# A feed-forward layer of inner width 682 in eleven tiles of up to 128 instead of twelve of 114, in a kernel whose engines follow orders written out by hand

## Chip, cores and metric

The kernel runs on one core of a Trainium2 chip, as one program. The metric is the time of one execution on the device in microseconds. Engines are called by the profile's names: PE (TensorE, with PEld for its weight loads), DVE (VectorE), ACT (ScalarE), POOL (GpSimd), SP (the queue that issues DMAs).

## What is computed

The input is x of shape 8 x 1024 x 256 in float32. A differential attention with 16 heads and a layer norm come first; the change doesn't touch them. Then follow two layers of local attention and gated feed-forward, and another layer norm. Cut to what matters:

```python
for l in range(2):
    h = shift_token(x)                       # half of the channels one token later
    q, k, v = split(h @ wqkv)                # 8 heads of 64
    q, k = rotary_xpos(l2norm(q) * q_scale, l2norm(k) * k_scale)
    x = x + local_attention(q, k, v) @ wo    # windows of 128 tokens, each sees itself and the one before
    h = shift_token(x)
    h = (h - mean) / sqrt(var + 1e-5) * ln_g + ln_b
    a, g = split(h @ w1 + b1)                # 256 -> 2 x 682
    x = x + (a * gelu(g)) @ w2 + b2          # 682 -> 256
```

682 is 6 x 113.67, or 5 x 128 + 42.

## The kernel before

The first half of the program (to about 2950 us of the span) is the differential attention. The second half walks 128 windows W of 128 tokens: 2 layers x 8 sequences x 8 windows. Four windows make a half sequence of 512 tokens, and the feed-forward of half m runs beside the attention of the four windows that follow it, spread by c = W % 4:

- c = 0: attention_out (8 matmuls, x = x + o @ wo), mean
- c = 1: variance, then gate tiles 0 to 5 (2 matmuls each, 256 = 2 x 128 rows of contraction)
- c = 2: hidden tiles 0 to 5 (2 matmuls each); ACT takes the gelu of the gates between two table loads, DVE multiplies (gated)
- c = 3: ffn_out (2 x 6 matmuls)

So windows 0 to 3 run with no feed-forward beside them, and the last half's feed-forward runs alone after window 127.

Beside this each window W does its attention: queries and keys of window W + 1 (PSUM banks 0 and 1), values of W, four head pairs hp of scores (banks 4 and 5), a maximum on DVE (largest), exp and sum on ACT (exps), a division on DVE (normalise), a transposition on PE (transpose_p, bank 3), a copy to SBUF on ACT (place_p), and the weighing of the values on PE (weigh, bank 6). Queries and keys of W + 1 are squared on ACT (squares), normed (DVE norms, ACT inverse_norms, POOL), rotated on DVE (rotate_own, rotate_other, combine), transposed on PE (transpose_q, transpose_k, again bank 3) and copied by ACT (place_q, place_k). In the first window of a sequence (W % 8 = 0) the keys are 128 instead of 256, so that scores, transpositions, copies and weighing have half the columns or half the calls.

Nothing schedules this: each engine runs its own attend(W) (PE from L945, ACT from L1366, DVE from L1782), a list of calls for each c, written out by hand, and every engine takes its list strictly in order. Waits are on semaphores. Those that matter here:

```python
pe.wait_ge(t_read, done(W * 6 + 2 + hp))     # transpose_p: ACT has copied bank 3 after the transposition before
pe.wait_ge(t_read, done(W * 6 + 1))          # transpose_k: place_q is done
pe.wait_ge(t_read, done(W * 6 + 2))          # scores(W, 0): place_k of this window is done
pe.wait_ge(p_ready, done(W * 4 + hp + 1))    # transpose_p: DVE's normalise
pe.wait_ge(xsum_done, done(m + 1))           # mean: POOL has summed the two residuals
pe.wait_ge(hn_done, done(2 * m + 2))         # gate 0: scale_bias on ACT
```

Feed-forward results and values take turns in PSUM banks 7 and 2: fbank(use) gives the bank of the use-th result of a half, 22 uses in a half. gate (L892) writes ps[0:114], gate_out on ACT (L1338) copies it with the bias to gates, gelu works in place, hidden (L912) writes ps[0:114], gated on DVE (L1761) adds the bias and multiplies, ffn_out (L929) contracts 114 rows at a time. w1 lies as [128, 2, 2, 6, 114], w2 as [114, 6, 256], padded from 682 to 684.

Of the kernel before, what the change touches and what calls it, by code (L numbers as in the profile page):

```python
# [6 lines left out]
F32 = mybir.dt.float32  # L7
# [32 lines left out]
HP = -(-HID // HB)  # L40
# [3 lines left out]
def done(n):  # L44

    return n + START
# [70 lines left out]
def fbank(use):  # L117

    return 2 if use % 2 else 7


V_USE = (0, 5, 12, 19)
# [7 lines left out]
def program(nc, d, nb):  # L130

    assert nb % 2 == 0
    with ExitStack() as ctx:
# [79 lines left out]
        w1 = sb("w1", [P, 2, 2, HB, HP], F32)  # L213
        w2 = sb("w2", [HP, HB, 256], F32)
# [3 lines left out]
        b1 = sb("b1", [HP, 2, HB], F32)  # L218
# [20 lines left out]
        gb_ = sb("gates", [HP, HB, 512], F32)  # L239
        hh = sb("hh", [HP, HB, 512], F32)  # L240
# [299 lines left out]
        def _(pe):  # L540
# [319 lines left out]
            def attention_out(m, oc, fs, beside):  # L860
# [19 lines left out]
            def mean(m):  # L880
# [3 lines left out]
                pe.matmul(ps[:, fbank(3), :], mean_w[:], both[:, 0, :], start=True, stop=True).then_inc(fm_full, 1)  # L884

            def variance(m):
# [3 lines left out]
                pe.matmul(ps[:, fbank(4), :], mean_w[:], both[:, 1, :], start=True, stop=True).then_inc(fv_full, 1)  # L890

            def gate(m, j, beside, kcs=(0, 1)):  # L892
# [14 lines left out]
                for kc in kcs:  # L907
                    mmi = pe.matmul(ps[0:HP, fbank(6 + j), :], w1[:, kc, 1, j, :], cn[:, kc, :], start=kc == 0, stop=kc == 1)  # L908
# [3 lines left out]
            def hidden(m, j, beside, kcs=(0, 1)):  # L912
# [11 lines left out]
                for kc in kcs:  # L924
                    mmi = pe.matmul(ps[0:HP, fbank(13 + j), :], w1[:, kc, 0, j, :], cn[:, kc, :], start=kc == 0, stop=kc == 1)  # L925
# [3 lines left out]
            def ffn_out(m, oc, js, beside):  # L929
# [7 lines left out]
                for j in js:  # L937
                    mmi = pe.matmul(ps[:, fbank(20 + oc), :], w2[:, j, oc * P:(oc + 1) * P], hh[:, j, :],  # L938
# [4 lines left out]
            def attend(W):  # L943
                m, c = half_of(W), W % 4
                if c == 0:  # L945
# [16 lines left out]
                    attention_out(m, 1, (1,), True)  # L962
                    weigh(W, 0)
                    weigh(W, 1)
                    transpose_p(W, 2)
                    attention_out(m, 1, (2,), True)
                    transpose_p(W, 3)
                    attention_out(m, 1, (3,), True)
                    transpose_q(W + 1)
                    weigh(W, 2)  # L970
                    weigh(W, 3)
                    transpose_k(W + 1)
                    mean(m)
                    scores(W + 1, 0)
                elif c == 1:
                    queries(W + 1, 0)
                    queries(W + 1, 1)
                    scores(W, 1)
                    keys(W + 1, 0)
                    variance(m)  # L980
                    keys(W + 1, 1)
                    transpose_p(W, 0)
                    scores(W, 2)
                    values(W, 0)
                    values(W, 1)
                    transpose_p(W, 1)
                    scores(W, 3)
# [3 lines left out]
                    weigh(W, 0)  # L991
                    weigh(W, 1)
                    transpose_p(W, 2)
# [3 lines left out]
                    transpose_p(W, 3)  # L997
                    gate(m, 3, True, (0,))
                    gate(m, 3, True, (1,))
                    gate(m, 4, True, (0,))  # L1000
                    gate(m, 4, True, (1,))
                    transpose_q(W + 1)
                    gate(m, 5, True, (0,))
# [1088 lines left out]
```

## Time and profile before

| what | us |
|---|---|
| median of 3 runs (6137.58 to 6144.04) | 6137.9 |
| the profiled execution's own time | 6143.95 |
| its span, first to last instruction | 6141.9 |
| PE busy | 5830.0 (95%) |
| DVE busy | 4145.9 (68%) |
| ACT busy | 3460.2 (56%) |
| POOL busy | 910.1 (15%) |
| mean granted TensorE clock | 0.983 |

The span is what lies between the first and the last instruction; the execution's own time has some 2 us more. Busy shares are averages over both halves of the program. The end of a matmul is modelled, so that busy time of PE tells less than the distance between starts. A timeline row merges a run of like instructions: start, duration of the run, engine, line, operation, names, shapes, xcount, and in brackets the idle time before it and what ended it. A float32 matmul makes two records (x2); a transposition of a head pair makes four, a scores call four, a weigh call eight. "issue" is time in which an engine waited for nothing that the profile shows.

### The profile page before, as it was taken

Reading aid. Unit: us, or ns where it says so; the run is one execution under the profiler, and the core shown is the slowest. Engines: PE = TensorE matmul, PEld = TensorE weight load, DVE = VectorE, ACT = ScalarE, POOL = GpSimd, SP = SyncE. Lnnn points to the kernel's source line nnn. Section 1 sums busy time; section 2 is a strip of 40 time slices with the busy share of each in tenths; the row PEclk is TensorE's granted clock in tenths of the full one; section 3 lists DMA queues with packets and bytes.
Section 4 is the critical chain, followed back from the end, with each engine's and each line's share of the span. In section 5 each row is a group of like instructions: output and inputs, shape, how many; then the busy total and the mean of one; then the engine's idle time right before and its main releaser. Section 6 shows DMA issues by size and latency. Waiting matters only on the chain.

```text
span 6141.9 us, 146596 instructions
## 1 busy us (share of the span) xinstructions
PE 5830.0 (95%) x58112; PEld 2637.5 (43%) x58112; DVE 4145.9 (68%) x10780; ACT 3460.2 (56%) x6980; POOL 910.1 (15%) x1873
## 2 busy tenths in 40 slices
PE   8999999999999999998699999999999999999985
PEld 3343434344343434433344444444444444444432
DVE  5777777777777777775566666666666666666633
ACT  4666666666666666665355555555555555555532
POOL 2222222222222222211000000000000000000000
PEclk9999999999999999999799999999999999999997
DMA  3333333332323333231100000000000000000004
GB/s 67 52 52 61 52 61 51 57 57 49 66 51 62 51 56 57 48 60 33 64 8 14 15 8 14 14 8 15 12 27 15 11 11 15 11 11 15 11 28 144
DMA packets 137129, 232.17 MB, mean 38 GB/s; under 512 B 40476, under 2 KB 40604, under 8 KB 135680
## 3 DMA queue, kind: packets, MB, share of 16 engines
q1 hardware_dynamic: 136448, 222.83, 17.5%
q8 instruction: 460, 7.54, 0.5%
q14 instruction: 221, 1.81, 0.1%
HBM read 53.86 MB, written 33.55 MB: 14 GB/s over the span
## 4 chain that ended last, share of the span: by engine, by line
PE 81%; issue 6%; DVE 6%; ACT 4%; DMA 2%; POOL 1%; SPq 0%; POOLq 0%; ACTq 0%; DVEq 0%
PE ps L548 21%; PE ps L677 14%; PE ps L769 12%; PE ps L908 5%; PE ps L938 5%; PE ps L925 5%; PE ps L835 5%; PE ps L855 4%; PE ps L843 4%; ACT pt L1179 3%; DVE mc L1542 2%; PE ps L875 2%; PE ps L813 1%; PE ps L822 1%; DVE junk L1538 1%
## 5 line engine op out<-in xcount | busy, mean ns | idle before, releaser
L1179 ACT ACTIVATE pt<-ps 128x1024 f32<-128x1024 f32 (+7 forms) x2048 | 1235.7, 652 | 747.5 <-PE ps L548 525.5
L1538 DVE CUSTOM_DVE_ANT_0 junk<-ps,causal 128x128 bf16<-128x128 f32 (+3 forms) x2048 | 989.2, 487 | 439.7 <-PE ps L548 422.7
L548 PE MATMUL ps<-kt,qt 96*32 96x512 bf16 (+3 forms) x12288 | 1066.9, 332 | 100.0 <-DVE mc L1542 55.8
L677 PE MATMUL ps<-pt,ones 128*32 128x512 f32 (+3 forms) x6144 | 1151.1, 489 | 0.0
L677 PE MATMUL ps<-pt,vs 128*32 128x512 f32 (+3 forms) x3072 | 1147.6, 489 | 0.0
L677 PE MATMUL ps<-pt,va 128*32 128x512 f32 (+3 forms) x3072 | 1144.2, 487 | 0.5 <-POOL pt L1952 0.4
L548 PE MATMUL ps<-qt,kt 98*32 98x512 bf16 (+3 forms) x12288 | 827.9, 328 | 42.0 <-ACT pt L1179 32.7
L769 PE MATMUL ps<-wqkv,xs 128*128 128x512 f32 x1536 | 786.1, 621 | 13.8 <-DMA wqkv<-in_wqkv 13.8
L1542 DVE TENSOR_REDUCE mc<-ps 128x1 f32<-128x512 f32 x1024 | 704.8, 688 | 99.7 <-PE ps L548 77.0
L1952 POOL TENSOR_SCALAR_AFFINE_SELECT pt<-pt 128x256 f32<-128x256 f32 x1024 | 454.9, 444 | 2139.2 <-ACT pt L1179 2139.2
L548 PEld LDWEIGHTS ps<-kt,qt 96*32 96x32 bf16 x12288 | 347.9, 94 | 893.9 <-DVE mc L1538 429.4
L1301 ACT ACTIVATE sm<-sm,mxw 128x256 f32<-128x256 f32 (+1 forms) x1024 | 495.4, 485 | 335.0 <-DVE mxw L1719 334.6
L1719 DVE CUSTOM_DVE_ANT_0 sm<-ps,window 128x256 f32<-128x256 f32 (+1 forms) x1024 | 375.7, 405 | 321.9 <-PE ps L835 320.2
L1309 ACT ACTIVATE ptw<-ps 128x512 f32<-128x512 f32 (+1 forms) x512 | 287.4, 561 | 442.5 <-PE ps L843 413.4
L548 PEld LDWEIGHTS ps<-qt,kt 98*32 98x32 bf16 x12288 | 331.1, 96 | 337.4 <-issue 161.1
L677 PEld LDWEIGHTS ps<-pt,va 128*32 128x32 f32 x3072 | 320.0, 109 | 311.3 <-issue 187.1
L1979 POOL TENSOR_TENSOR nt<-rn 128x16 f32<-128x16 f32 x128 | 44.2, 345 | 2403.9 <-ACT rn L1278 2403.9
L769 PEld LDWEIGHTS ps<-wqkv,xs 128*128 128x128 f32 x1536 | 257.8, 191 | 276.6 <-issue 269.0
L938 PE MATMUL ps<-hh,w 114*128 114x512 f32 x768 | 363.5, 597 | 0.9 <-DVE hh L1768 0.9
L908 PE MATMUL ps<-cn,w 128*114 128x512 f32 x768 | 354.8, 599 | 4.4 <-ACT cn L1335 4.4
L925 PE MATMUL ps<-cn,w 128*114 128x512 f32 x768 | 358.0, 596 | 0.8 <-ACT gates L1345 0.8
L835 PE MATMUL ps<-kp,qp 64*128 64x256 f32 (+1 forms) x2048 | 348.7, 417 | 7.0 <-DVE mxw L1719 4.2
(147 smaller groups left out, 8570.0 us busy)
## 6 DMA issues: line engine op xcount, KB each, us to landing
qt<-part SPq DMA_DIRECT2D x768, 64.0 KB, 2.4
kt<-part SPq DMA_DIRECT2D x768, 64.0 KB, 2.5
ya<-wy SPq DMA_DIRECT2D x128, 128.0 KB, 2.3
yb<-wy SPq DMA_DIRECT2D x128, 128.0 KB, 2.3
xs<-between_phases SPq DMA_DIRECT2D x32, 512.0 KB, 3.9
between_phases<-xo SPq DMA_DIRECT2D x32, 512.0 KB, 2.8
xt<-in_x SPq DMA_DIRECT2D x16, 512.0 KB, 6.0
between_phases<-z SPq DMA_DIRECT2D x16, 512.0 KB, 2.8
```

The source lines that it names most:

```text
L548: mmi = pe.matmul(ps[32 * q:32 * q + 32, bank, lo:hi], weights[:, 32 * q:32 * q + 32], moving, start=start, stop=stop)
L677: mmi = pe.matmul(ps[32 * q:32 * q + 32, 4 + half, lo - half * 512:hi - half * 512], w, probs(kb)[:, i, lo - first(kb):hi - first(kb)], st ...
L769: return pe.matmul(ps[:, bank, :], xs[:, kc, at:at + P], wqkv[l][:, kc, n * 512:n * 512 + 512], start=kc == 0, stop=kc == 1)
L835: pe.matmul(ps[:, 4 + q, 0:n], qp[rows, hp, :], kp[rows, hp, :, :].rearrange("p a k -> p (a k)")[:, 0:n], start=True, stop=True).then_inc( ...
L908: mmi = pe.matmul(ps[0:HP, fbank(6 + j), :], w1[:, kc, 1, j, :], cn[:, kc, :], start=kc == 0, stop=kc == 1)
L925: mmi = pe.matmul(ps[0:HP, fbank(13 + j), :], w1[:, kc, 0, j, :], cn[:, kc, :], start=kc == 0, stop=kc == 1)
L938: mmi = pe.matmul(ps[:, fbank(20 + oc), :], w2[:, j, oc * P:(oc + 1) * P], hh[:, j, :], start=j == 0, stop=j == HB - 1)
L1179: act.activation(probs(kb)[:, i, kb * P - first(kb):1024 - first(kb)], ps[:, 2 * i:2 * i + 2, :].rearrange("p a q -> p (a q)")[:, kb * P:1 ...
L1301: i = act.activation(sm[:, hp, q, 0:n], sm[:, hp, q, 0:n], ACT.Exp, scale=-1.0, bias=mxw[:, hp, q:q + 1], accum_out=sumw[:, hp, q:q + 1])
L1538: ins = dve.tensor_tensor_reduce(out=junk[:, bank - 6, 0:w], in0=ps[:, bank, 0:w], in1=causal[:, 512 - w:512], scale=1.0, scalar=NEG, op0= ...
L1542: ins = dve.reduce_max(into, ps[:, bank, 0:w], AX_X)
L1952: pool.affine_select(out=diag, in_=diag, compare_op=ALU.is_ge, fill=0.0, base=0, pattern=[[0, 2], [1, P]], channel_multiplier=-1).then_inc ...
```

## The change

The inner width is cut into 5 tiles of 128 and one of 42. The five full tiles have a gate and a hidden matmul pair each as before. The last tile has its 42 hidden values and its 42 gates in one tile of w1: hidden values on rows 0 to 41, gates on rows 64 to 105 (HPAIR = 106), so that one pair of matmuls makes both; it is called gate 5, and hidden 5 is gone. ACT copies all 106 rows with their bias, takes the gelu of rows 64 to 105 into a tile of its own (glast, rows 0 to 41), and DVE multiplies the two in SBUF. ffn_out contracts 128 rows five times and 42 rows once. A half has now 21 results in PSUM, an odd number, so the turn of the banks depends on m as well. b1, w1 and w2 are laid out on the host to match.

Cut to its core (the changes of fbank's arguments and of the layout on the host are left out):

```diff
-HP = -(-HID // HB)
+HLAST = HID - (HB - 1) * P
+HPAIR = 64 + HLAST
...
-def fbank(use):
-
-    return 2 if use % 2 else 7
...
-V_USE = (0, 5, 12, 19)
+def fbank(m, use):
+
+    return 2 if (m + use) % 2 else 7
...
+V_USE = (0, 5, 12, 18)
...
-        w1 = sb("w1", [P, 2, 2, HB, HP], F32)
-        w2 = sb("w2", [HP, HB, 256], F32)
+        w1 = sb("w1", [P, 2, 2 * HB - 1, P], F32)
+        w2 = sb("w2", [P, HB, 256], F32)
...
                 for kc in kcs:
-                    mmi = pe.matmul(ps[0:HP, fbank(6 + j), :], w1[:, kc, 1, j, :], cn[:, kc, :], start=kc == 0, stop=kc == 1)
+                    if j < HB - 1:
+                        mmi = pe.matmul(ps[:, fbank(m, 6 + j), :], w1[:, kc, j, :], cn[:, kc, :], start=kc == 0, stop=kc == 1)
+                    else:
+                        mmi = pe.matmul(ps[0:HPAIR, fbank(m, 6 + j), :], w1[:, kc, 2 * HB - 2, 0:HPAIR], cn[:, kc, :],
+                                        start=kc == 0, stop=kc == 1)
...
                 for j in js:
-                    mmi = pe.matmul(ps[:, fbank(20 + oc), :], w2[:, j, oc * P:(oc + 1) * P], hh[:, j, :],
+                    rows = slice(0, P if j < HB - 1 else HLAST)
+                    mmi = pe.matmul(ps[:, fbank(m, 19 + oc), :], w2[rows, j, oc * P:(oc + 1) * P], hh[rows, j, :],
                                     start=j == 0, stop=j == HB - 1)
...
-            for j in range(HB):
+            for j in range(HB - 1):
                 hidden(m, j, False)
...
+                if j < HB - 1:
+                    act.activation(gb_[:, j, :], gb_[:, j, :], ACT.Gelu).then_inc(ge_done, 1)
+                else:
+                    act.activation(glast[:, :], gb_[64:HPAIR, j, :], ACT.Gelu).then_inc(ge_done, 1)
...
+                if j < HB - 1:
+                    dve.wait_ge(a_full, done(m * (HB - 1) + j + 1))
+                    dve.scalar_tensor_tensor(hh[:, j, :], ps[:, fbank(m, 13 + j), :], b1[:, HB - 1 + j:HB + j], gb_[:, j, :],
+                                             ALU.add, ALU.mult).then_inc(hh_done, 1)
+                else:
+                    dve.tensor_tensor(hh[0:HLAST, j, :], gb_[0:HLAST, j, :], glast[:, :], ALU.mult).then_inc(hh_done, 1)
...
```

The lists of calls of PE, ACT and DVE are written anew for all four c. On DVE, in c = 3, heads_out and output change places at the end, so that the two outputs come first. Three places of the built programs show the rest.

PE at the end of c = 0, from the last attention_out (L875, in the change L877) to the first scores of the next window (L835, L837). L843/L845 is transpose_p, L855/L857 weigh (x4 for each head pair), L813/L815 transpose_q, L822/L824 transpose_k, L884/L886 the mean. Before:

```order
L875 MATMUL ps<-ot,wo 128x512 x5
L855 MATMUL ps<-ptw,vt 64x128 x8
L843 MATMUL ps<-identf,sm 128x128 x4
L875 MATMUL ps<-ot,wo 128x512
L843 MATMUL ps<-identf,sm 128x128 x4
L875 MATMUL ps<-ot,wo 128x512
L813 MATMUL ps<-identf,rr 128x128 x4
L855 MATMUL ps<-ptw,vt 64x128 x8
L822 MATMUL ps<-identf,rr 128x128 x4
L884 MATMUL ps<-both,mean_w 128x512
L835 MATMUL ps<-kp,qp 128x256 x2
```

And in the change:

```order
L877 MATMUL ps<-ot,wo 128x512 x8
L845 MATMUL ps<-identf,sm 128x128 x4
L857 MATMUL ps<-ptw,vt 64x128 x8
L845 MATMUL ps<-identf,sm 128x128 x4
L857 MATMUL ps<-ptw,vt 64x128 x4
L815 MATMUL ps<-identf,rr 128x128 x4
L886 MATMUL ps<-both,mean_w 128x512
L824 MATMUL ps<-identf,rr 128x128 x4
L857 MATMUL ps<-ptw,vt 64x128 x4
L837 MATMUL ps<-kp,qp 128x256 x2
```

The eight attention_out matmuls now stand together, the mean has moved between the two last transpositions, and between transpose_p 3 and transpose_q, and between transpose_k and the scores, there is one weigh call and no 512-column matmul.

PE in the second half of c = 2, from the last long run of hidden matmuls on (L925, in the change L931). Before:

```order
L925 MATMUL ps<-cn,w_93 114x512 x3
L855 MATMUL ps<-ptw,vt 64x128 x8
L843 MATMUL ps<-identf,sm 128x128 x4
L925 MATMUL ps<-cn,w_93 114x512
L843 MATMUL ps<-identf,sm 128x128 x4
L925 MATMUL ps<-cn,w_93 114x512
L813 MATMUL ps<-identf,rr 128x128 x4
L855 MATMUL ps<-ptw,vt 64x128 x8
L822 MATMUL ps<-identf,rr 128x128 x4
L925 MATMUL ps<-cn,w_93 114x512
L835 MATMUL ps<-kp,qp 128x256 x2
```

And in the change:

```order
L931 MATMUL ps<-cn,w_93 128x512 x3
L857 MATMUL ps<-ptw,vt 64x128 x4
L845 MATMUL ps<-identf,sm 128x128 x4
L931 MATMUL ps<-cn,w_93 128x512 x2
L845 MATMUL ps<-identf,sm 128x128 x4
L857 MATMUL ps<-ptw,vt 64x128 x4
L845 MATMUL ps<-identf,sm 128x128 x4
L857 MATMUL ps<-ptw,vt 64x128 x4
L815 MATMUL ps<-identf,rr 128x128 x4
L931 MATMUL ps<-cn,w_93 128x512
L824 MATMUL ps<-identf,rr 128x128 x4
L857 MATMUL ps<-ptw,vt 64x128 x4
```

Hidden 5 is gone. Two gaps between transpositions (2 and 3, 3 and q) that held a hidden matmul now hold a weigh call of one head pair (x4), and one such call stands between transpose_k and the scores.

ACT in c = 2, from the inverse norms on: L1350/L1359 and L1360/L1372 are the table loads, L1356/L1366 and L1368 gelu, L1309/L1314 place_p, L1301/L1306 exps (x2 a head pair). Before:

```order
L1278 ACTIVATE rn_108<-lnn 128x16
L1350 ACT_TABLE_LOAD
L1356 ACTIVATE gates<-gates 114x512 x5
L1309 ACTIVATE ptw<-ps 128x512
L1356 ACTIVATE gates<-gates 114x512
L1360 ACT_TABLE_LOAD
L1301 ACTIVATE sm,sumw<-sm,mxw 128x256 x2
L1309 ACTIVATE ptw<-ps 128x512
L1301 ACTIVATE sm,sumw<-sm,mxw 128x256 x2
L1309 ACTIVATE ptw<-ps 128x512 x2
L1289 ACTIVATE qp<-ps 128x512
L1295 ACTIVATE kp<-ps 128x4x128
```

And in the change:

```order
L1283 ACTIVATE rn_108<-lnn 128x16
L1359 ACT_TABLE_LOAD
L1366 ACTIVATE gates<-gates 128x512
L1314 ACTIVATE ptw<-ps 128x512
L1366 ACTIVATE gates<-gates 128x512 x4
L1368 ACTIVATE glast<-gates 42x512
L1372 ACT_TABLE_LOAD
L1306 ACTIVATE sm,sumw<-sm,mxw 128x256 x4
L1314 ACTIVATE ptw<-ps 128x512 x3
L1294 ACTIVATE qp<-ps 128x512
L1300 ACTIVATE kp<-ps 128x4x128
```

place_p 0 has moved ahead of five gelus, and exps 3 ahead of place_p 1, so that the three copies after it stand together.

## Rows read from the trace of the kernel before

**Rows 1.** Busy time of TensorE, from the page.

```profile
PE 5830.0 (95%) x58112; PEld 2637.5 (43%) x58112; DVE 4145.9 (68%) x10780; ACT 3460.2 (56%) x6980; POOL 910.1 (15%) x1873
```

**Rows 2.** Stretches: us, busy PE, PEld, DVE, ACT, POOL, clock, DMA.

```profile
4340.94:4362.57 21.63, 21.63 (x104) 10.54 (x103) 14.84 (x36) 9.44 (x26) 2.98 (x5) 1.00 0.15 48
4362.57:4387.01 24.44, 24.44 (x113) 12.12 (x111) 14.85 (x35) 16.51 (x37) 2.49 (x5) 1.00 0.01 2
4387.01:4410.91 23.90, 23.90 (x111) 11.29 (x109) 17.29 (x39) 15.32 (x34) 0.86 (x4) 1.00 0.01 1
4410.91:4434.41 23.50, 23.50 (x110) 11.71 (x108) 14.25 (x35) 9.63 (x26) 0.86 (x4) 1.00 0.00 1
```

**Rows 3.** Timeline of PE in c = 0.

```profile
4343.48 1.12 PE L769 MATMUL ps<-wqkv,xs 128*128 128x512 f32 x2
4344.54 0.70 PE L835 MATMUL ps<-kp,qp 64*128 64x256 f32 x4
...
4350.41 4.46 PE L875 MATMUL ps<-ot,wo 128*128 128x512 f32 x10
4354.80 1.09 PE L855 MATMUL ps<-ptw,vt 128*64 128x128 f32 x16
4355.82 0.66 PE L843 MATMUL ps<-identf,sm 128*128 128x128 f32 x4
4356.32 1.02 PE L875 MATMUL ps<-ot,wo 128*128 128x512 f32 x2
4357.26 0.63 PE L843 MATMUL ps<-identf,sm 128*128 128x128 f32 x4
4357.72 1.02 PE L875 MATMUL ps<-ot,wo 128*128 128x512 f32 x2
```

**Rows 4.** Timeline of all engines at the end of c = 2.

```profile
4404.41 0.66 PE L843 MATMUL ps<-identf,sm 128*128 128x128 f32 x4
...
4405.10 0.60 ACT L1309 ACTIVATE ptw<-ps 128x512 f32<-128x512 f32 x1 [1.53 <-PE ps L843]
4405.81 0.42 PEld L843 LDWEIGHTS ps<-identf,sm 128*128 128x128 f32 x4 [0.73 <-issue]
...
4408.83 0.66 PE L822 MATMUL ps<-identf,rr 128*128 128x128 f32 x4
...
4409.52 0.60 ACT L1295 ACTIVATE kp<-ps 128x512 f32<-128x512 f32 x1 [1.01 <-PE ps L822]
4410.27 0.30 PEld L835 LDWEIGHTS ps<-kp,qp 64*128 64x128 f32 x4 [0.77 <-ACT kp L1295]
```

**Rows 5.** Timeline of all engines around the mean, in a sequence's first window.

```profile
4450.21 0.69 DVE L1742 TENSOR_TENSOR xm<-ps,xs 128x512 f32<-128x512 f32 x1 [1.25 <-PE ps L875]
...
4450.98 1.27 POOL L1991 TENSOR_TENSOR both<-xm 128x512 f32<-128x512 f32 x1 [5.66 <-DVE xm L1742]
...
4452.30 1.12 PE L884 MATMUL ps<-both,mean_w 128*128 128x512 f32 x2 [0.35 <-POOL both L1991]
```

**Rows 6.** Groups by line, 3400 to 5800 us: the hidden matmuls.

```profile
L925 PE MATMUL ps<-cn,w 128*114 128x512 f32 x624 | 291.4, 596 | 0.0
```

**Rows 7.** Timeline of ACT in c = 2 (window from 4387.01).

```profile
4394.69 1.28 ACT L1350 ACT_TABLE_LOAD   x1
4395.99 2.71 ACT L1356 ACTIVATE gates<-gates 114x512 f32<-114x512 f32 x5
...
4401.01 0.51 ACT L1301 ACTIVATE sm<-sm,mxw 128x256 f32<-128x256 f32 x1
...
4402.01 0.57 ACT L1309 ACTIVATE ptw<-ps 128x512 f32<-128x512 f32 x1
```

**Rows 8.** Groups by line, 3400 to 5800 us: variance to normed input.

```profile
L1335 ACT ACTIVATE cn<-cn,lnp 128x512 f32<-128x512 f32 x52 | 39.6, 808 | 0.0
L1758 DVE TENSOR_TENSOR cn<-cn,rlf 128x1024 f32<-128x1024 f32 x26 | 31.9, 1225 | 11.5 <-ACT rlf L1327 11.5
L1325 ACT ACTIVATE rlf<-ps,eps_c 128x512 f32<-128x512 f32 x26 | 17.9, 688 | 0.2 <-PE ps L890 0.2
```

More of the change, by code:

```diff
@@ L883, in mean @@
                 pe.wait_ge(xsum_done, done(m + 1))
-                pe.matmul(ps[:, fbank(3), :], mean_w[:], both[:, 0, :], start=True, stop=True).then_inc(fm_full, 1)
+                pe.matmul(ps[:, fbank(m, 3), :], mean_w[:], both[:, 0, :], start=True, stop=True).then_inc(fm_full, 1)
             def variance(m):
@@ L978, in attend @@
                     scores(W, 1)
+                    variance(m)
+                    values(W, 0)
+                    values(W, 1)
+                    scores(W, 2)
                     keys(W + 1, 0)
-                    variance(m)
                     keys(W + 1, 1)
                     transpose_p(W, 0)
[L983 to L987, printed above, removed]
                     gate(m, 0, True, (0,))
@@ L996, in attend @@
                     gate(m, 2, True, (1,))
-                    transpose_p(W, 3)
+                    transpose_p(W, 1)
+                    scores(W, 3)
+                    weigh(W, 0)
+                    weigh(W, 1)
                     gate(m, 3, True, (0,))
+                    transpose_p(W, 2)
                     gate(m, 3, True, (1,))
@@ L1011, in attend @@
                     queries(W + 1, 1)
+                    keys(W + 1, 0)
+                    keys(W + 1, 1)
+                    scores(W, 1)
+                    values(W, 0)
+                    values(W, 1)
+                    hidden(m, 0, True, (0,))
+                    hidden(m, 0, True, (1,))
+                    scores(W, 2)
+                    transpose_p(W, 0)
+                    hidden(m, 1, True, (0,))
+                    hidden(m, 1, True, (1,))
+                    scores(W, 3)
+                    hidden(m, 2, True, (0,))
+                    hidden(m, 2, True, (1,))
+                    hidden(m, 3, True, (0,))
+                    weigh(W, 0)
+                    transpose_p(W, 1)
+                    hidden(m, 3, True, (1,))
+                    hidden(m, 4, True, (0,))
+                    transpose_p(W, 2)
+                    weigh(W, 1)
+                    transpose_p(W, 3)
+                    weigh(W, 2)
+                    transpose_q(W + 1)
+                    hidden(m, 4, True, (1,))
+                    transpose_k(W + 1)
+                    weigh(W, 3)
+                    scores(W + 1, 0)
+                else:
+                    queries(W + 1, 0)
+                    queries(W + 1, 1)
+                    values(W, 0)
                     scores(W, 1)
```

225 lines of the change are left out of this document (100 added, 125 removed).

## The prediction, made before the change was run

> **What bounds the kernel now.** I read the page's busy shares first: TensorE is busy 5830.0 of 6141.9 us, every other engine far less [rows 1]. A share this high can hide waits, so the view that decides is the table of stretches cut at the start of successive windows of the second half [rows 2]. There PE is busy for all of 21.63, 24.44, 23.90 and 23.50 us, at a granted clock of 1.00 (full speed, 2.4 GHz), while VectorE (DVE) has 14 to 17 us and ScalarE (ACT) 9 to 17 us of work. One feed-forward half takes four such windows, some 93 us, and 31 of the 32 halves run beside windows. The end of a matmul is modelled, though, so a busy PE may still be waiting, and only the spacing of starts tells what one call costs.
>
> That spacing is in the timeline of PE [rows 3]. One 512-column matmul (two records) is 0.86 us: five of them take 4.39 us (4350.41 to 4354.80), the last stretched 0.09 by what follows. Scores (64 rows) and weigh (64 columns) use part of the array; crossing to or from the other kind costs about 0.1 us: a 512-column matmul between two scores calls takes 1.06 (4343.48 to 4344.54), 0.2 more than inside a run. Two head pairs of weigh take 1.02 (4354.80 to 4355.82); with the records read singly 0.49 are the first's and 0.54 the last's. A transpose group costs 0.50 after weigh (4355.82 to 4356.32) and 0.46 to 0.44 after a matmul (4357.26 to 4357.72). Pricing both orders with these spacings, as if nothing waited, gives for full windows c = 0 to 3 of before 21.15, 24.43, 23.67 and 23.67 us, 92.9 together; measured were 21.63, 24.44, 23.90 and, with the cheap first scores of a sequence, 23.50 (that saves 0.21). So before waits nearly 0.5 in c = 0 and 0.2 in c = 2, and hardly elsewhere. Counting the windows at a sequence's start, whose transposes are half as long, that is about 0.9 us in a half.
>
> What are the waits? **All transposes share bank 3.** The round trip is in [rows 4]: transposes start at 4404.41, ACT copies from 4405.10 for 0.60, the next transposes' weights load at 4405.81. So two transpose groups start at least 1.43 apart after weigh, 1.38 after a matmul (4355.82 to 4357.26 is 1.44 with one matmul between, which itself then took 0.94). The keys' transposes at 4408.83, copied at 4409.52, let the next scores load at 4410.27, the same distance. One 512-column matmul between two transposes almost covers the trip; one weigh call (0.54) doesn't. The other wait is the mean in c = 0: DVE's second residual at 4450.21, the POOL sum at 4450.98, the matmul at 4452.30, with PE idle 0.35 by its own row [rows 5].
>
> **The change, part by part.**
>
> 1. Hidden tile 5 is gone, two matmuls in a half: 2 x 0.86 = 1.72 us, in 32 halves 55 us. Columns streamed set the price, so tiles of 128 instead of 114 values cost the same (the hidden group of before, on 114 columns, has 596 ns a record [rows 6], and spaces its matmuls at 0.86 like attention_out on 128), and ffn_out keeps its twelve matmuls.
>
> 2. Waitless spacing of the new order. Runs of scores or weigh calls stay 23 in a half, but three pairs of weigh calls are pulled apart (3 x 0.05), and at two borders a matmul stands where a transpose stood (2 x 0.05): +0.25. Priced as before: 21.20, 24.28, 22.21, 23.77, together 91.46, which is 1.46 less.
>
> 3. Round trips of bank 3 in the new order.
>  - c = 0 ends transpose_p 3, weigh 2, transpose_q, mean, transpose_k, weigh 3, scores. The spacing to transpose_q would be 0.55 + 0.54 = 1.09 and must be 1.43: wait 0.34. To transpose_k 0.50 + 0.86: wait 0.08. From transpose_k to scores 0.53 + 0.54 = 1.07 against 1.38: wait 0.31. Sum 0.73, where before had nearly 0.5 (one-matmul trips and the mean). The mean is no longer late: the eight attention_out calls end about 15.7 us into the window, two residuals of 0.69 and the sum of 1.27 end by 18.4, and the mean is due at 18.9.
>  - c = 1: transpose_p 3, one matmul, transpose_q, one matmul, transpose_k: 2 x 0.08.
>  - c = 2 ends transpose_p 2, weigh 1, transpose_p 3, weigh 2, transpose_q, hidden 4, transpose_k, weigh 3, scores: 0.31 + 0.34 + 0.08 + 0.31 = 1.04, where before had 0.2.
>  - c = 3: transpose_p 1, one matmul, transpose_p 2: 0.08.
>  With these the windows are 21.93, 24.44, 23.25 and 23.85 against 21.63, 24.44, 23.90 and 23.71: +0.30, 0, -0.65, +0.14. At a sequence's start (every other c = 0) the transposes are half as long and I get +0.15 for +0.30. Sum in a half: -0.28 us. **Of the 1.46 us of spacing won, 1.2 come back as waits of a transpose for a copy.**
>
> 4. Matmul ffn_out 5 now contracts 42 rows. No row of before has a 512-column matmul on so few. The nearest from one side is ffn_out on 114 rows, which passes as a full one (0 added), from the other the scores on 64 rows, which pay 0.1 at each border. 42 rows fit in 64, so I take the second: once it stands between two transposes (+0.09, +0.1 and +0.05, less the 0.08 wait of c = 3, which it covers), once ahead of scores (its border only moves). I take +0.2 in a half; ends 0 and 0.4. The Trainium skill, page TensorEngine Tiling (Array Packing), under Tiling Modes, says that changing the tiling mode, not just the tile, drains TensorE, and has a 64-row mode for contractions up to 64. By that rule the sum has this term, by the 114-row row alone it has not and would end 6 us lower.
>
> 5. ACT and DVE queues. In c = 2 exps 3 moves ahead of place_p 1 [rows 7]. From the first table load ACT must do 1.3 + six gelus at 0.54 + a copy 0.57 + 1.3 + two exps at 1.0 + the copy 0.57 = 9.0 us; the load began 7.7 us into the window before (4394.69 less 4387.01) and may begin 7.2 to 7.7 now, so the copy ends by 16.7 and transpose_p 2 is due at 16.97: covered, with 0.2 us to spare. In c = 1 the variance ends at 3.6; ln and exp (0.69 and much the same), divide (1.23) and two scalings of 0.81 with four handovers of 0.1 end at 8.2 or just before [rows 8], and gate 0 is due at 8.2: 0, at most 0.1. In c = 3 heads_out now stands behind output 1, so the next window's first maximum starts 0.7 late; scores 1 waits for it and is due 0.3 after it ends. POOL and SP get no new work; each weight load is a few kB larger and off the path. All at nothing; if a cover is gone, its microseconds go straight to PE.
>
> 6. The last half, after the windows, has no other work on PE: -1.7. Windows 0 to 3 carry no feed-forward work, 88 us of latency in a new order: 0, plus or minus 2.
>
> Sum: 31 x (-0.28 + 0.2) - 1.7 = -4.2 us. The profiled execution took 6143.95 (span 6141.9), the median of the runs is 6137.9; taken from each, 6139.8 and **6133.7**. I call a difference under 0.2% (12.3 us) no change, about what a measurement of this kernel can tell.
>
> **The rivals.**
> - *Faster: the trips are mostly hidden.* If the waits stay at before's 0.9 us a half (a copy of ACT sooner than [rows 4] have it, or PE loading weights during the trip), the gain is 31 x 1.46 + 1.7 = 47 us: 6091. If half of the new waits fall away and ffn_out 5 costs nothing, 31 x (0.28 + 0.6) + 1.7 = 29: 6109. For it: PE was full before. Against: the trip reads the same at each place. Chance of ending over 12 us faster: 0.30.
> - *Slower: ACT's queue in c = 2.* Everything from gelu 1 to exps 3 now stands ahead of place_p 1 in one queue, and transposes 2, 3, q and k and the next scores hang on it one after another. Beyond 0.2 to 0.3 us of delay it is paid whole: 1 us late is 0.7 x 31 = 22 us, so 6155. For it: the table load waits for norms on DVE behind others. Against: ACT idled over 1 us twice in that window before. Chance 0.22, with the other covers of step 5, which would show alike.
> - *The 42-row matmuls pass as full ones*: 31 x (-0.28) - 1.7 = -10.4, so 6127.5. That lies inside my own case and decides no sign alone.
>
> No change gets 0.48. Its own range is 6126 to 6150, and to hold 8 in 10 I reach to the half-way faster case and the late-ACT case: 6109 to 6156.
>
> **What the profile after would show.** Gate records 640 on 128 columns and 128 on 106, hidden 640 instead of 768, ffn_out 640 on 128 rows and 128 on 42. Window lengths cut at the wqkv matmuls: 21.9, 24.4, 23.2 and 24.0. In c = 0 and c = 2 the starts of transpose_p 3 and transpose_q 1.43 apart with one weigh call between, and transpose_k to scores 1.38. ffn_out 5: its transposes 0.53 and 0.50 if it switches the array, 0.44 if not. Wrong would be: c = 2 near 22.2 (trips hidden), transpose_p 2 in c = 2 later than 17.2 us after the window's start with ACT busy until then (the queue), or a c = 3 longer than 24.3.

## The result: 6149.8 us against 6139.6, slightly slower

| what | before | change |
|---|---|---|
| median of 20 runs, us | 6139.64 (6136.98 to 6144.04) | 6149.8 (6143.82 to 6157.67) |
| ratio, 95% interval | | 1.0016 [1.001, 1.0023] |
| profiled execution / its span, us | 6143.95 / 6141.9 | 6148.83 / 6146.8 |
| PE busy, us | 5830.0 | 5796.8 |
| mean granted clock | 0.983 | 0.985 |

PE works 33 us less by the profile's count, and the program takes 5 us more of span and 10 us more in the median. The stretches that answer to [rows 2] say where. This is the view of stretches of the change, cut at the first matmul of five successive windows: c = 0 to 3, and the c = 0 window that starts a sequence. The columns are the stretch, its us, and the busy us of PE, PEld, DVE, ACT and POOL, the granted clock, the DMA share and GB/s.

```profile
4341.25:4363.58 22.33, 21.63 (x103) 10.61 (x103) 15.91 (x38) 9.81 (x27) 3.27 (x5) 1.00 0.14 48
4363.58:4388.04 24.46, 24.46 (x112) 12.15 (x110) 14.10 (x34) 16.42 (x37) 2.13 (x5) 1.00 0.00 1
4388.04:4411.15 23.11, 22.63 (x106) 10.97 (x104) 16.92 (x39) 15.74 (x35) 0.86 (x4) 1.00 0.01 1
4411.15:4435.08 23.93, 23.93 (x111) 11.88 (x109) 13.24 (x34) 9.47 (x26) 1.95 (x4) 1.00 0.00 1
4435.08:4455.15 20.07, 19.14 (x80) 8.94 (x79) 14.18 (x38) 8.11 (x27) 3.10 (x5) 1.00 0.22 78
```

c = 2, which lost two matmuls (1.72 us), is 0.79 us shorter. c = 3 is 0.43 longer, c = 0 is 0.70 longer, and a sequence's first window 0.49 (20.07 against the 19.58 that the trace of before has from 4434.41 to 4453.99). But for a few single windows the lengths repeat to 0.02 us through the second half; c = 3 is 0.42 longer where full scores follow. In a pair of halves that is 0.70 + 0.49 - 2 x 0.79 + 2 x 0.42 + 2 x 0.02 = +0.49 us, 7.5 us over 15.5 pairs. Three single windows of before (4, 45 and 126) are together 3.8 us longer than their like and one of the change 0.3, so that windows 4 to 126 take 3.9 us more. The rest of the span's +4.9 lies around them: the second half starts 2.0 us earlier in this execution, windows 0 to 3 take 1.1 us more, and what lies behind the start of window 127 takes 2.0 us more.

The median moved by 10 us and these two executions by 5, because the one of before lies 4.3 us above its median and the one of the change 1.0 below. A single execution doesn't tell a few microseconds: over all thirteen kept traces the second half starts between 2949 and 2956 us, though the change and the edits below leave the differential attention alone. The window lengths carry the argument from here on.

The wait that I had not seen stands in c = 0. This is the timeline of all engines in the change's c = 0, from transpose_p 2 (L845) over weigh (L857), transpose_q (L815), the mean (L886) and transpose_k (L824) to the next scores (L837):

```profile
4356.85 0.60 PE L845 MATMUL ps<-identf,sm 128*128 128x128 f32 x4
...
4357.38 1.10 PE L857 MATMUL ps<-ptw,vt 128*64 128x128 f32 x16
...
4358.15 0.60 ACT L1314 ACTIVATE ptw<-ps 128x512 f32<-128x512 f32 x1 [5.50 <-PE ps L857]
...
4358.89 0.63 PE L845 MATMUL ps<-identf,sm 128*128 128x128 f32 x4 [0.41 <-ACT ptw L1314]
4359.44 0.42 PEld L857 LDWEIGHTS ps<-ptw,vt 128*64 128x64 f32 x8 [0.17 <-issue]
...
4360.29 0.63 PE L815 MATMUL ps<-identf,rr 128*128 128x128 f32 x4 [0.19 <-ACT ptw L1314]
...
4360.76 1.02 PE L886 MATMUL ps<-both,mean_w 128*128 128x512 f32 x2
...
4361.61 0.65 PE L824 MATMUL ps<-identf,rr 128*128 128x128 f32 x4
...
4362.19 0.66 PE L857 MATMUL ps<-ptw,vt 128*64 128x128 f32 x8
...
4362.95 0.30 PEld L837 LDWEIGHTS ps<-kp,qp 64*128 64x128 f32 x4 [0.34 <-ACT kp L1300]
```

transpose_q follows transpose_p 3 by 1.40 us, and the scores follow transpose_k by 1.34: the trips of [rows 4], near the 1.43 and 1.38 that were forecast. But transpose_p 3 follows transpose_p 2 by 2.04 us, though two weigh calls stand between them and only 1.43 is the trip. The bracket behind the copy at 4358.15 names who let it go: not the transposes (L845) but weigh (L857).

### The profile page after: what moved, and what is told of

Its sections match the earlier page's. It is cut to its first block, busy times and chain, and to the rows that moved or that the text cites. A ratio compares the mean times of both kernels' runs of the same rounds, so it can differ in the third digit from the quotient of the medians.

```text
span 6146.8 us, 146308 instructions
## 1 busy us (share of the span) xinstructions
PE 5796.8 (94%) x57984; PEld 2631.9 (43%) x57984; DVE 4118.5 (67%) x10780; ACT 3477.9 (57%) x6980; POOL 948.9 (15%) x1873
## 4 chain that ended last, share of the span: by engine, by line
PE 81%; DVE 6%; ACT 5%; issue 5%; DMA 2%; SPq 0%; POOL 0%; POOLq 0%; ACTq 0%; DVEq 0%
PE ps L550 21%; PE ps L679 14%; PE ps L771 12%; PE ps L945 6%; PE ps L837 5%; PE ps L911 5%; PE ps L931 4%; PE ps L845 4%; PE ps L877 3%; PE ps L857 3%; ACT pt L1184 3%; DVE mc L1554 2%; PE ps L815 1%; ACT ptw L1314 1%; PE ps L824 1%
## 5 line engine op out<-in xcount | busy, mean ns | idle before, releaser
L771 PE MATMUL ps<-wqkv,xs 128*128 128x512 f32 x1536 | 768.8, 620 | 13.9 <-DMA wqkv<-in_wqkv 13.9
L1306 ACT ACTIVATE sm<-sm,mxw 128x256 f32<-128x256 f32 (+1 forms) x1024 | 495.4, 485 | 282.0 <-DVE mxw L1731 281.6
L1314 ACT ACTIVATE ptw<-ps 128x512 f32<-128x512 f32 (+1 forms) x512 | 289.6, 566 | 522.8 <-PE ps L845 319.6
L837 PE MATMUL ps<-kp,qp 64*128 64x256 f32 (+1 forms) x2048 | 362.6, 415 | 13.1 <-ACT kp L1300 6.1
L945 PE MATMUL ps<-hh,w 128*128 128x512 f32 (+1 forms) x768 | 371.6, 609 | 1.6 <-DVE hh L1784 1.6
L1741 DVE TENSOR_TENSOR sm<-sm,sumw 128x512 f32<-128x512 f32 (+1 forms) x512 | 337.0, 658 | 17.6
L845 PEld LDWEIGHTS ps<-identf,sm 128*128 128x128 f32 x1920 | 228.7, 142 | 276.1 <-issue 240.7
```

The costliest lines, as they stand in the source:

```text
L771: return pe.matmul(ps[:, bank, :], xs[:, kc, at:at + P], wqkv[l][:, kc, n * 512:n * 512 + 512], start=kc == 0, stop=kc == 1)
L837: pe.matmul(ps[:, 4 + q, 0:n], qp[rows, hp, :], kp[rows, hp, :, :].rearrange("p a k -> p (a k)")[:, 0:n], start=True, stop=True).then_inc( ...
L845: mmi = pe.transpose(ps[:, 3, (2 * q + a) * P:(2 * q + a + 1) * P], sm[:, hp, q, a * P:(a + 1) * P], identf[:])
L945: mmi = pe.matmul(ps[:, fbank(m, 19 + oc), :], w2[rows, j, oc * P:(oc + 1) * P], hh[rows, j, :], start=j == 0, stop=j == HB - 1)
L1306: i = act.activation(sm[:, hp, q, 0:n], sm[:, hp, q, 0:n], ACT.Exp, scale=-1.0, bias=mxw[:, hp, q:q + 1], accum_out=sumw[:, hp, q:q + 1])
```

## Experiments

Windows are given as c = 0, 1, 2, 3 and, after a semicolon, a sequence's first. Before: 21.63, 24.44, 23.90, 23.50; 19.58. The change: 22.33, 24.46, 23.11, 23.93; 20.07. "Before" is a run of the kernel before on the same chip; its median lay between 6139.3 and 6142.9.

### 1. The new tiles in the old lists

```diff
 (attend of PE, ACT and DVE as before)
-                    hidden(m, 5, True, (0,))
...
-                    hidden(m, 5, True, (1,))
```

> Eleven tiles, but PE, ACT and DVE keep the lists of before, with the two calls of hidden 5 struck out; the outputs are the same. Theory A (round trips through bank 3 bound the end of c = 2): the two matmuls stood between transpose_p 3 and transpose_q and between transpose_k and the scores, where the spacing was 1.40 and 1.44 us; without them the trips still take 1.38 to 1.43 each, so c = 2 stays at 23.8 us or more (23.9 before), the other windows stay as before but for ffn_out 5 (+0.1 to 0.3 in c = 3), and the time is 6137 to 6143. Rival B (matmul time is what counts): c = 2 falls by 1.5 to 1.7 to 22.3 and the time to about 6090.

Measured: 6155.36 us, ratio 1.0019 [1.0009, 1.0028]; windows 21.63, 24.46, 23.82, 23.88; 19.58. PE at the end of its c = 2 (L931 hidden, L845 transpose_p, L815 transpose_q, L857 weigh, L824 transpose_k, L837 scores):

```profile
4412.00 0.63 PE L845 MATMUL ps<-identf,sm 128*128 128x128 f32 x4
4413.41 0.63 PE L815 MATMUL ps<-identf,rr 128*128 128x128 f32 x4 [0.78 <-ACT ptw L1314]
4413.97 1.09 PE L857 MATMUL ps<-ptw,vt 128*64 128x128 f32 x16
4414.99 0.66 PE L824 MATMUL ps<-identf,rr 128*128 128x128 f32 x4
4416.34 0.70 PE L837 MATMUL ps<-kp,qp 64*128 64x256 f32 x4 [0.69 <-ACT kp L1300]
```

With nothing between them the transposes are 1.41 us apart, and the scores 1.35 behind transpose_k. Two matmuls are gone and c = 2 is only 0.08 us shorter. Theory A's windows hold, but for c = 3, which is 0.38 longer where 0.3 was the most it allowed. All of that is in one place: the 42-row matmul stands inside a run of five ffn_out matmuls there. The run before, and the same run here (ten records in one row, under the shape of the first):

```profile
4422.72 4.56 PE L938 MATMUL ps<-hh,w 114*128 114x512 f32 x10
4428.77 4.95 PE L945 MATMUL ps<-hh,w 128*128 128x512 f32 x10
```

From its start to the next transposes it is 4.39 us before and 4.79 here. The time came out 12 us above the range named for it, with the windows adding up to +0.6 us in a pair, 10 us; as in the change, the median is some microseconds over what the windows say. So the missing matmuls give almost nothing in the old lists, and what the new lists bring in c = 2 (0.7 us) is their own.

### 2. Queries' and keys' transposes in other banks

```diff
-                pe.wait_ge(t_read, done(W * 6))
...
-                    mmi = pe.transpose(ps[:, 3, hp * P:(hp + 1) * P],     # transpose_q
+                    mmi = pe.transpose(ps[:, 0, hp * P:(hp + 1) * P],
...
-                pe.wait_ge(t_read, done(W * 6 + 1))
...
-                    mmi = pe.transpose(ps[:, 3, hp * P:(hp + 1) * P],     # transpose_k
+                    mmi = pe.transpose(ps[:, 1, hp * P:(hp + 1) * P],
...
 (place_q reads bank 0, place_k bank 1)
```

> The changed kernel with transpose_q and transpose_k written to banks 0 and 1 (queries and keys, read by then) instead of bank 3, so that they need no copy to be done first; ACT copies from there. Theory A (trips of bank 3): the waits ahead of transpose_q (0.31 in c = 0 and 2) and transpose_k (0.08) go, the trip from transpose_k to the scores stays; transpose_k comes 0.3 to 0.4 earlier, c = 0 about 22.0, c = 1 about 24.3, c = 2 about 22.85, c = 3 unchanged, the time 22 us less, about 6128. Rival B (the wait ahead of transpose_q is for combine on DVE, or ACT's copies in their order set the scores anyway): windows change by less than 0.1 and the time by less than 4 us.

Measured: 6126.51 us, ratio 0.9976 [0.9966, 0.9986]; windows 22.05, 24.30, 22.84, 23.92; 19.79. Every window is within 0.05 of theory A. The end of its c = 2 on PE (L843 transpose_p, L855 weigh, L814 transpose_q, L929 hidden 4, L822 transpose_k, L835 scores):

```profile
4392.12 0.63 PE L843 MATMUL ps<-identf,sm 128*128 128x128 f32 x4 [0.19 <-ACT ptw L1312]
4392.68 0.66 PE L855 MATMUL ps<-ptw,vt 128*64 128x128 f32 x8
4393.26 0.66 PE L814 MATMUL ps<-identf,rr 128*128 128x128 f32 x4
4393.76 1.02 PE L929 MATMUL ps<-cn,w 128*128 128x512 f32 x2
4394.62 0.60 PE L822 MATMUL ps<-identf,rr 128*128 128x128 f32 x4
4395.15 0.66 PE L855 MATMUL ps<-ptw,vt 128*64 128x128 f32 x8
4395.90 0.70 PE L835 MATMUL ps<-kp,qp 64*128 64x256 f32 x4
```

transpose_p 3 to transpose_q is 1.14 instead of 1.40, and the bracket is gone. transpose_k to the scores is 1.28 with 1.07 of work in it: that trip stays, since the scores need the copied keys.

### 3. The same banks in the old lists

```diff
 (old_orders, with transpose_q and transpose_k in banks 0 and 1)
```

> Eleven tiles in the lists of before (as in old_orders), with transpose_q and k in banks 0 and 1. Theory A (in those lists too the trips of bank 3 swallow what hidden 5 gave back): transpose_p 3 to transpose_q falls from 1.41 to about 0.44, the trip from transpose_k to the scores stays at 1.34; c = 2 falls from 23.82 to about 22.9, c = 0 by 0.1, c = 1 and 3 stay, the time by 30 us against old_orders, to about 6125. Rival B (transpose_q there waits for combine on DVE): c = 2 stays above 23.5 and the time above 6145.

Measured: 6142.48 us, ratio 1.0006 [0.9996, 1.0015]; windows 21.63, 24.45, 23.66, 23.88; 19.58. Here theory A failed: c = 2 fell by 0.16, not 0.9, and the time to 6142, not to 6125. Rival B's window (above 23.5) held, its time (above 6145) did not. transpose_q (L814) still starts 1.22 us behind transpose_p 3 at 4399.17, and its bracket names what it waits for:

```profile
4400.39 0.66 PE L814 MATMUL ps<-identf,rr 128*128 128x128 f32 x4 [0.59 <-DVE rr L1721]
```

L1721 is the last operation of combine on DVE, which in the old list stands behind normalise 3. So in the old lists two waits end within 0.2 us of each other, and sparing one leaves the other. In the new lists combine is early enough. The wait for combine was read from the trace; no run took it away by itself.

### 4. Is it normalise 3 that holds transpose_p 3?

My first reading of c = 0 was DVE's queue: combine idles 0.78 us there for POOL's norms, and normalise 3 stands behind it.

```diff
+                    normalise(W, 3)
                     combine(W + 1)
                     residual(m, 0)
-                    normalise(W, 3)
                     residual(m, 1)
```

> The changed kernel with one call moved on DVE in c = 0: normalise 3 ahead of combine and residual 0. Theory A (transpose_p 3 waits for normalise 3, which stands behind a combine that waits 0.8 us for POOL's norms): the 0.48 us wait ahead of transpose_p 3 goes, c = 0 falls from 22.33 to about 21.85 and a sequence's first window from 20.08 to about 19.6, the time by about 15 us to 6135. Rival B (the copy of bank 3 or the mean is the next to be late): c = 0 falls by less than 0.15, because the mean or transpose_q waits instead, and the time by less than 5 us.

Measured: 6150.18 us, ratio 1.001 [1.0001, 1.002]; windows 22.34, 24.46, 23.11, 23.92; 20.07. Nothing moved, so theory A fell. Rival B's number holds (less than 0.15), but not its reason, that the wait would move on to the mean or transpose_q: transpose_p 3 starts at the same point of the window, 17.64 us, as in the change. DVE's idle time was slack.

### 5. More buffers for the copied probabilities

The bracket at 4358.15 led to this. place_p(hp) writes ptw[hp % 2], the buffer that weigh(hp - 2) reads, so it waits for o_full. In the new c = 0 list weigh 0 stands behind transpose_p 2.

```diff
-        ptw = sb("ptw", [P, 2, 4, P], F32)
+        ptw = sb("ptw", [P, 4, 4, P], F32)
...
-                act.wait_ge(o_full, done(W * 4 + hp - 1))
+                act.wait_ge(o_full, done(W * 4 + hp - 3))
...
 (place_p and weigh use ptw[:, hp])
```

> The changed kernel with four instead of two SBUF buffers for the copied probabilities (ptw), so that place_p 2 and 3 need not wait for weigh 0 and 1. Theory A (in c = 0 weigh 0 now stands behind transpose_p 2, and the copy after transpose_p 2 waits for it because it writes weigh 0's buffer; transpose_p 3 waits for that copy): transpose_p 3 starts 1.55 instead of 2.04 us after transpose_p 2, c = 0 falls from 22.33 to 21.85 and a sequence's first window from 20.08 to 19.6, the other windows stay within 0.05, the time falls by 15 us to about 6135. Rival B (something else holds transpose_p 3, normalise 3 or the plain trip of bank 3): c = 0 stays within 0.1 and the time within 4 us.

Measured: 6138.91 us, ratio 0.9997 [0.9988, 1.0006]; windows 21.88, 24.46, 23.12, 23.92; 19.63. The same place in its timeline, from transpose_p 2 to transpose_p 3:

```profile
4349.57 0.60 PE L845 MATMUL ps<-identf,sm 128*128 128x128 f32 x4
...
4350.10 1.09 PE L857 MATMUL ps<-ptw,vt 128*64 128x128 f32 x16
4350.21 0.60 ACT L1314 ACTIVATE ptw<-ps 128x512 f32<-128x512 f32 x1 [4.84 <-PE ps L845]
...
4351.12 0.66 PE L845 MATMUL ps<-identf,sm 128*128 128x128 f32 x4
```

The copy now starts 0.64 us after the transposes and is let go by them (L845); transpose_p 3 follows by 1.55. c = 0 and a sequence's first window fall by 0.45 and 0.44. This one wait cost about what the whole change lost: without it the change is level with before.

### 6. The other way to take it away

```diff
                     attention_out(m, 1, (2,), True)
-                    attention_out(m, 1, (3,), True)
-                    transpose_p(W, 2)
                     weigh(W, 0)
                     weigh(W, 1)
+                    transpose_p(W, 2)
+                    attention_out(m, 1, (3,), True)
                     transpose_p(W, 3)
```

> The changed kernel with weigh 0 and 1 ahead of transpose_p 2 in c = 0, and the last attention_out matmul between transpose_p 2 and 3: the order that before had there, without a further buffer. Theory A (the copy after transpose_p 2 waited for weigh 0): transpose_p 3 follows transpose_p 2 by 1.43 instead of 2.04 us, c = 0 falls by 0.35 to 21.98 and a sequence's first window by about the same, the time by about 11 us to 6139. Rival B (mean or combine is next): c = 0 falls by less than 0.1.

Measured: 6158.0 us, ratio 1.0028 [1.0018, 1.0038]; windows 22.39, 24.46, 23.12, 23.92; 20.55. Its c = 0 (transpose_p 2 and 3, transpose_q, the mean):

```profile
4364.53 0.66 PE L845 MATMUL ps<-identf,sm 128*128 128x128 f32 x4
...
4365.97 0.63 PE L845 MATMUL ps<-identf,sm 128*128 128x128 f32 x4
4366.09 0.69 DVE L1754 TENSOR_TENSOR xm<-ps,xs 128x512 f32<-128x512 f32 x1 [0.95 <-PE ps L877]
...
4366.85 1.27 POOL L2006 TENSOR_TENSOR both<-xm 128x512 f32<-128x512 f32 x1 [4.45 <-DVE xm L1754]
4367.37 0.63 PE L815 MATMUL ps<-identf,rr 128*128 128x128 f32 x4 [0.19 <-ACT ptw L1314]
...
4368.18 1.12 PE L886 MATMUL ps<-both,mean_w 128*128 128x512 f32 x2 [0.18 <-POOL both L2006]
```

transpose_p 3 does follow by 1.44 (theory A), but the last attention_out matmul is 1.6 us later, and residual, sum and mean behind it; the mean now waits for POOL (rival B). c = 0 is 0.06 us longer than in the change, and a sequence's short first window 0.48. The wait was traded for the next one, at a loss of 8 us by the windows; the two ratios' intervals overlap.

### 7. ffn_out 5 over all rows

```diff
-                    rows = slice(0, P if j < HB - 1 else HLAST)
+                    rows = slice(0, P)
...
+            pool.memset(hh[:, HB - 1, :], 0.0).then_inc(k2_ready, 1)
```

> The changed kernel with ffn_out 5 contracting 128 rows, of which 86 are zeros (set once); all else is the same. Theory A (42 rows switch the array to its 64-row form): the transposes ahead of and behind ffn_out 5 cost 0.44 and 0.53 instead of 0.53 and 0.59, the matmul between them 0.94 (the trip) instead of 1.05, so c = 3 falls by about 0.25 to 23.87, and the time by 8 us to about 6142; at the second ffn_out 5 nothing, because it overlaps the scores now and would not then. Rival B (42 rows run like 114): no window changes by more than 0.03, time the same within 3 us.

Measured: 6143.43 us, ratio 1.0003 [0.9994, 1.0013]; windows 22.34, 24.47, 23.11, 23.70; 20.08. The change around its first ffn_out 5, and its second:

```profile
4423.63 0.60 PE L845 MATMUL ps<-identf,sm 128*128 128x128 f32 x4
4424.16 1.12 PE L945 MATMUL ps<-hh,w 42*128 42x512 f32 x2
4425.21 0.66 PE L845 MATMUL ps<-identf,sm 128*128 128x128 f32 x4
4425.80 1.09 PE L857 MATMUL ps<-ptw,vt 128*64 128x128 f32 x16
...
4432.85 1.65 PE L945 MATMUL ps<-hh,w 128*128 128x512 f32 x3
4433.81 0.49 PE L837 MATMUL ps<-kp,qp 64*128 64x128 f32 x2
4434.34 0.59 PE L945 MATMUL ps<-hh,w 42*128 42x512 f32 x1
```

And the kernel with 128 rows at the first:

```profile
4423.75 0.60 PE L845 MATMUL ps<-identf,sm 128*128 128x128 f32 x4
4424.19 1.02 PE L945 MATMUL ps<-hh,w 128*128 128x512 f32 x2
4425.13 0.63 PE L845 MATMUL ps<-identf,sm 128*128 128x128 f32 x4
4425.69 1.09 PE L857 MATMUL ps<-ptw,vt 128*64 128x128 f32 x16
```

From the transposes to the weigh call it is 2.17 us with 42 rows and 1.94 with 128, of which 86 are zeros. Contracting a third of the rows made the piece dearer, and c = 3 falls by 0.23 when the rows are filled up.

### 8. All three together

```diff
 (the edits of 2, 5 and 7)
```

> The changed kernel with the three edits together: transpose_q and k in banks 0 and 1, four ptw buffers, ffn_out 5 over 128 rows. If the three waits are separate, as theory A has it, their gains add: windows c = 0 to 3 of 21.58, 24.30, 22.84 and 23.91, a sequence's first of 19.3, 2.85 us less in a pair of halves than the change, so 44 us less than it and about 37 us less than before: a ratio of 0.994. Rival B (one wait hides another): c = 0 stays at 21.9 or more because the mean waits for POOL, and the sum is short by 5 us or more.

Measured: 6104.0 us, ratio 0.9939 [0.9925, 0.9952]; windows 21.60, 24.30, 22.83, 23.70; 19.59. The gains add, save 0.3 us in a sequence's first window; no window is over its forecast by more. It is faster than both kernels.

### 9. The same buffers under the kernel before

```diff
 (before.py with the edits of 2 and 5)
```

> The kernel before, twelve tiles and its own lists, with transpose_q and k in banks 0 and 1 and four ptw buffers. Theory A (its lists put a 512-column matmul into each trip, so there is hardly a wait to take away, and what bounds it is matmul time): c = 2 falls by 0.08 to 23.82, the others by 0.05 or less, the time by about 3 us, ratio 0.9995. Then the gain of all_three is owed to the missing matmuls as well as to the buffers. Rival B (the buffers alone make the gain of all_three): windows fall by 1 us in a pair or more and the time by 15 us or more.

Measured: 6135.95 us, ratio 0.9993 [0.9983, 1.0003]; windows 21.63, 24.43, 23.80, 23.51; 19.58. Only c = 2 moved, by 0.10, as theory A has it. So the 36 us of all_three aren't owed to the buffers alone: they come from fewer matmuls once the waits that had taken their place are gone.

### 10. transpose_k at once behind transpose_q

```diff
 (all_three; in c = 0 and c = 2)
                     transpose_q(W + 1)
-                    mean(m)                  # c = 2: hidden(m, 4, True, (1,))
                     transpose_k(W + 1)
+                    mean(m)                  # c = 2: hidden(m, 4, True, (1,))
                     weigh(W, 3)
```

> all_three with transpose_k straight behind transpose_q in c = 0 and c = 2 (the mean, and the second matmul of hidden 4, after it). Theory A (the last wait in these windows is the copy between transpose_k and the next scores, 0.22 us each): c = 0 falls from 21.60 to about 21.4, a sequence's first from 19.60 to 19.4, c = 2 from 22.84 to 22.6, the time by 12 us more, to about 6092. Rival B (what follows is late anyway: combine for transpose_q, or the later hidden 4 delays gated 4 and 5, heads_out and the next maxima on DVE): c = 2 or the c = 3 behind it doesn't fall, and the time stays within 4 us of 6104.

Measured: 6094.63 us, ratio 0.993 [0.9913, 0.9946]; windows 21.43, 24.48, 22.67, 23.69; 18.96. c = 0 and 2 fall as theory A has it, and a sequence's first window by 0.63, more than it; c = 1 behind them takes back 0.18, and 0.4 behind a sequence's first window, for which no cause was looked for. By the windows it is 9 us faster than all_three, whose ratio's interval overlaps its own; it has the lowest median of the versions that were run.

### 11. POOL beside DVE

```diff
                     rotate_own(W + 1)
-                    rotate_other(W + 1)
                     normalise(W, 2)
+                    rotate_other(W + 1)
                     combine(W + 1)
```

> The changed kernel with rotate_other behind normalise 2 instead of ahead of it on DVE in c = 0. A look at POOL's four small operations on the norms, which took 0.51, 1.08, 0.20 and 0.22 us there, the long ones ending just after a DVE tensor_tensor on SBUF alone. Theory A (a POOL operation waits while such a DVE operation runs, not while DVE reads PSUM): with rotate_other, which reads PSUM, running at their start, the first two take 0.2 each and the third or fourth, beside combine, about 1. Rival B (they are slow for another reason): the second still takes about 1. The windows stay as they are, 22.33 in c = 0, because nothing that PE waits for depends on it.

Measured: windows 22.33, 24.46, 23.11, 23.92; 20.07, as expected; one execution of 6153.18 us says no more. The timeline of POOL and DVE, in a sequence's first window:

```profile
4444.89 1.28 DVE L1710 TENSOR_TENSOR rr<-ps,tab 128x512 f32<-128x512 f32 x2
...
4445.61 0.21 POOL L1994 TENSOR_TENSOR nt<-rn 128x16 f32<-128x16 f32 x1 [16.87 <-ACT rn L1283]
4445.90 0.22 POOL L1996 TENSOR_TENSOR nt<-nt,rn 128x16 f32<-128x16 f32 x1
...
4446.20 1.22 DVE L1719 TENSOR_TENSOR rr<-ra,rr 128x1024 f32<-128x1024 f32 x1
4446.21 1.28 POOL L1998 TENSOR_SCALAR nt<-nt 128x16 f32<-128x16 f32 x1
```

Beside a DVE operation that reads PSUM (L1710) POOL's take 0.2 us; the one that starts with combine's addition (L1719), which has both operands in SBUF, takes 1.28 and ends 0.07 us after it. That is theory A.

## Why the prediction was wrong

I forecast no change, 4 us less; it was 10 us more, 0.16%. That lies inside the range, but on the other side of zero than the sum, and the interval (0.1 to 0.23% more) leaves zero out. Step by step:

- **Steps 1 and 2** (matmul time, -1.46 us in a half) held as spacing: c = 1, which has hardly a wait, took 24.46 against 24.44 forecast. old_orders shows that this time is not the time of the kernel.
- **Step 3, c = 2**: forecast 23.25, measured 23.11. The trips are there, transpose_p 3 to transpose_q 1.40 and transpose_k to the scores 1.33 instead of 1.43 and 1.38. qk_banks took the waits of transpose_q and transpose_k away and got 0.27 us there, less than the 0.34 + 0.08 that this step has for them.
- **Step 3, c = 0: this is the step that failed.** Forecast 21.93, measured 22.33; a sequence's first window 19.73 against 20.07. I counted the two weigh calls between transpose_p 2 and 3 as cover for the trip, and did not ask whether the copy in that trip had another condition. It had: weigh 0 itself, which the new list puts behind transpose_p 2, frees the copy's target. The wait of 0.49 us before transpose_p 3 (2.04 less 1.55) is my error there, and ptw4 removes it: 21.88 and 19.63, within 0.1 of the forecast. In 15.5 pairs it is 0.45 + 0.44 each, 14 us by the windows, and 0.19% or 12 us by the ratios (1.0016 to 0.9997); from 4 us less to 10 us more I was off by 14. That the numbers match so well is in part luck: against my own windows c = 0 and a sequence's first missed by 0.40 + 0.34, 11 us in all, c = 2 gave 4 us back, c = 3 took 2 more, and step 6 was off as well.
- **Step 4** (42 rows): forecast +0.2 us in a half from the 64-row side, ends 0 and 0.4. Measured with ffn128: 0.23. (c = 3 without it is 0.19 longer than before, where step 3 has 0.14.) The rule of the Trainium skill on the drain at a change of tiling mode (page TensorEngine Tiling (Array Packing), under Tiling Modes) agrees with this: the transposes ahead of the 42-row matmul take 0.53 instead of 0.44. What I had not seen is at the second one, below, and that the price hangs on the neighbours: 0.40 inside a run of ffn_out matmuls in old_orders.
- **Step 5** (ACT and DVE queues): held where I looked. transpose_p 2 in c = 2 doesn't wait; the cover on ACT was enough. The late first maximum after c = 3 cost nothing on PE.
- **Step 6**: windows 0 to 3 took 1.1 us more (inside plus or minus 2). The last half's -1.7 did not come: from the start of window 127 to the end it is +2.0 in these two executions. The hidden matmuls there took 10.45 instead of 11.49 us, 1.04 less and not 1.7, but window 127 in its new order took 2.3 us more up to attention_out, and attention_out 10.92 instead of 9.23 up to the mean, at a granted clock of 0.84 instead of 1.00. Its rows before and in the change:

```profile
5913.45 7.10 PE L875 MATMUL ps<-ot,wo 128*128 128x512 f32 x16 [0.94 <-DVE xo L1779]
5918.68 8.79 PE L877 MATMUL ps<-ot,wo 128*128 128x512 f32 x16 [1.49 <-DVE ot L1747]
```

  The gates took 0.5 us more, at 0.82 instead of 0.85. The last ffn_out matmul starts 4.1 us later in all (ffn_out itself is 0.6 longer), and what follows it took 2.1 less. ptw4 shows the same slow attention_out, ffn128 and all_three don't; why the clock was lower is not shown.

Of the rivals, neither faster nor the ACT queue came. The slower side was reached by a wait of the same kind, on another resource and in another window.

## What to carry to other kernels

When a matmul is removed from a list in which engines wait for one another in turn, first ask what it was covering: here two matmuls of 0.86 us were worth 0.08 us, because they stood where PE would otherwise have waited, for round trips through a shared bank and, hardly later, for combine on DVE. For each wait that a reordering shortens, list all conditions of every instruction in the loop, the freeing of the target buffer as well as the arrival of the data: moving a consumer behind the next producer makes a double buffer single. Buffers and fewer matmuls were worth something only together: the two buffer edits alone gave 3 us, which the interval doesn't tell from nothing, and the change alone cost 10; with the filled rows all of it gave 36 us.

## What the runs showed of the hardware that I had not expected

- **A matmul on few rows and the next one in the list can overlap.** In the change's second ffn_out 5 (rows 0 to 41) and the scores behind it (two matmuls, on rows 0 to 63 and 64 to 127), the first two of the four records of scores start from 4433.81 on, 0.5 us before the last record of the 42-row matmul (4434.34), the other two behind it. That those two are the matmul on rows 64 to 127 is inferred; the trace doesn't name the rows. Where full scores follow, the pair takes 1.49 us and in ffn128 1.59, but the first 42-row record follows ffn_out 4 by 0.52 us instead of 0.43; from ffn_out 4 to the next window it is 2.44 us in both. What the switch costs there is given back whole.
- **A small POOL operation ends just after the DVE operation beside it, if that one reads and writes SBUF alone.** Of the change's 508 operations on the norms in the second half 95 take 0.33 to 1.31 us instead of 0.2, and each of these ends 0.06 to 0.08 us after such a DVE operation; none that ran wholly beside a DVE operation on PSUM takes over 0.23. It cost nothing here, and was my first, wrong suspect. (The profile's spans on POOL are rough.)
- A 512-column matmul on 42 rows is nowhere cheaper than one on 128. Between two groups of transposes it costs 0.23 us more, inside a run of full matmuls 0.40 more (old_orders, 4.79 against 4.39 with 114 rows before; no run fills the rows up there), and ahead of scores nothing.
